# All expert pages inside the last 64 steps of a GRU, and a dense tail for the last 256 tokens

## The reference, cut to what matters

```
B, T, D = 4, 1024, 1024;  E = 8 experts, rank 128, top 2
h = cond_2048                                     # [4, 1024]
for t in range(1024):                             # GRU cell
    gi = x[:, t] @ W_ih + b_ih;  gh = h @ W_hh + b_hh
    r, z = sigmoid(i_r + h_r), sigmoid(i_z + h_z)
    n = tanh(i_n + r * h_n);     h = (1 - z) * n + z * h;   hs[:, t] = h
logits = hs / norm(hs) @ router_w                 # 4096 tokens
combine = top-2 of softmax(logits), renormalised, else 0    # [4096, 8]
out = x + sum_e combine[:, e] * (hs @ Wa[e] @ Wb[e])         # Wa 1024x128, Wb 128x1024
```

## Time and profile before

| | us |
|---|---|
| median of the runs | 9897.77 |
| the profiled execution | 9896.98 |
| its span, first to last instruction | 9895.2 |
| the last step's state stands (L865) | 9692.03 |
| from there to the end of the span | 203.2 |

### The profile page before, as it was taken

The page is one execution under the profiler, slowest core; times in us unless marked ns, Lnnn a source line. Parts: engine busy times, 40 slices in busy tenths (PEclk is TensorE's granted clock), DMA queues, the critical chain, the costliest instruction groups (busy, mean ns, idle before and its releaser), DMA issues.

```text
span 9895.2 us, 527046 instructions
## 1 busy us (share of the span) xinstructions
PE 9695.6 (98%) x229320; PEld 7286.9 (74%) x229320; DVE 5543.4 (56%) x29383; ACT 1236.8 (12%) x4796; POOL 512.9 (5%) x1207
## 2 busy tenths in 40 slices
PE   7999999999999999999999999999999999999995
PEld 5897778666788967767678887667888667769663
DVE  5555555555555555555555555555555555555662
ACT  2111111111111111111111111111111111111111
POOL 1000000000000000000000000000000000000001
PEclk9999999999999999999999999999999999999997
DMA  7121222212222122222223222222222222222225
GB/s 170 42 46 45 47 50 46 46 40 50 48 45 51 41 47 69 60 67 60 63 59 67 60 61 65 58 64 60 65 62 61 61 67 62 59 64 58 62 56 148
DMA packets 1425751, 606.69 MB, mean 61 GB/s; under 512 B 853856, under 2 KB 1377632, under 8 KB 1423392
## 3 DMA queue, kind: packets, MB, share of 16 engines
q1 hardware_dynamic: 1397792, 490.53, 21.8%
q0 software_dynamic: 25616, 82.18, 3.6%
HBM read 435.31 MB, written 164.96 MB: 61 GB/s over the span
## 4 chain that ended last, share of the span: by engine, by line
PE 94%; DVE 2%; DMA 2%; issue 1%; ACT 0%; SPq 0%; POOL 0%; DVEq 0%; POOLq 0%; ACTq 0%
PE gh_ps L1055 78%; PE gi_ps L1077 13%; DMA out<-w_hh_parts 1%; PE y_ps L1112 1%; PE y_ps L1124 1%; PE route_ps L1088 1%; DMA w_ih_tile<-in_L_cond_W_ih 1%; DVE gh L814 1%; DVE gh_sum L820 0%; ACT gate L976 0%; ACT cand L979 0%; DVE pre L827 0%; DVE zn L847 0%; DVE r_cand L835 0%; DVE cand_in L838 0%
## 5 line engine op out<-in xcount | busy, mean ns | idle before, releaser
L1055 PE MATMUL gh_ps<-w_hh_parts,h_parts 128*12 128x288 bf16 (+1 forms) x196608 | 8418.2, 326 | 41.6 <-DVE h_parts L865 23.0
L1055 PEld LDWEIGHTS gh_ps<-w_hh_parts,h_parts 128*12 128x12 bf16 x196608 | 6068.5, 88 | 2016.8 <-DVE h_parts L865 99.8
L814 DVE STREAM_TRANSPOSE gh<-gh_ps 128x288 f32<-128x288 f32 (+1 forms) x2048 | 1193.5, 583 | 2512.4 <-PE gh_ps L1055 2509.3
L1077 PE MATMUL gi_ps<-x_t,w_ih_tile 128*32 128x256 f32 x24576 | 1727.2, 380 | 41.6 <-DMA w_ih_tile<-in_L_cond_W_ih 41.6
L976 ACT ACTIVATE gate<-pre 128x24 f32<-128x24 f32 (+1 forms) x2048 | 471.1, 230 | 7291.2 <-DVE pre L827 7291.2
L1077 PEld LDWEIGHTS gi_ps<-x_t,w_ih_tile 128*32 128x32 f32 x24576 | 957.7, 110 | 410.3 <-DMA w_ih_tile<-in_L_cond_W_ih 47.4
L835 DVE TENSOR_TENSOR r_cand<-h_cand,gate 128x12 f32<-128x12 f32 (+1 forms) x2048 | 361.7, 177 | 602.8 <-ACT gate L976 602.8
L820 DVE TENSOR_REDUCE gh_sum<-gh 128x36 f32<-128x108 f32 (+1 forms) x2048 | 651.0, 318 | 71.1
L847 DVE TENSOR_TENSOR zn<-one_minus_z,cand 128x12 f32<-128x12 f32 (+1 forms) x2048 | 361.0, 176 | 412.3 <-ACT cand L979 396.1
L979 ACT ACTIVATE cand<-cand_in 128x12 f32<-128x12 f32 (+1 forms) x2048 | 441.7, 216 | 1110.1 <-DVE cand_in L838 1110.1
L860 DVE TENSOR_TENSOR h_parts<-shared,h_parts 128x12 bf16<-128x12 f32 (+1 forms) x2048 | 360.1, 176 | 162.9 <-DVE shared L855 14.0
(11 more groups left out here) (111 smaller groups left out, 1820.1 us busy)
## 6 DMA issues: line engine op xcount, KB each, us to landing
w_ih_tile<-in_L_cond_W_ih SPq DMA_DIRECT2D x1544, 128.0 KB, 2.9
gi_scratch<-gi_stage SPq DMA_DIRECT2D x384, 128.0 KB
gi<-gi_scratch SPq DMA_DIRECT2D x256, 192.0 KB, 4.4
x_raw<-expert_rows_of_h SPq DMA_DIRECT2D x220, 128.0 KB
shared<-wa_by_partition SPq DMA_DIRECT2D x55, 512.0 KB
expert_b<-in_L_ffn_Wb SPq DMA_DIRECT2D x55, 512.0 KB
x_raw<-in_x SPq DMA_DIRECT2D x272, 64.0 KB, 2.9
window_rows<-shared SPq DMA_DIRECT2D x132, 128.0 KB, 2.3
```

Source lines behind the costliest of these rows:

```text
L814: nc.vector.transpose(gh[k][:, :, :, :], ps[k][sp_][:, 0:GATES * n * Q].rearrange("p (q c i) -> p q c i", q=GATES, i=Q))\
L1055: ins = nc.tensor.matmul(ps[k_out][t % 2][j * Q:j * Q + SPLIT * B, 0:GATES * (o1 - o0) * Q], h_parts[:, (t - 1) % 2, c, :, :].rearrange("p ...
L1077: ins = nc.tensor.matmul(ps_i[m % 2][j * Q:(j + 1) * Q, 0:COLS], w_i[m % slots][:, c, j * Q:(j + 1) * Q], x_t[:, c, :, :].rearrange("p t b ...
```

## The change

Block 15 works off 23 pages in the place of ten: 15 that may be full (`ND`) and the 8 partly filled ones. They alternate between two sets of tiles (`set_of`: `raws`, `hts`, `was`, `wbs`, `uss`, `yrows`, `banks`; the second set lies in tiles that have no other use in that block). A piece of one page may now stand in the same step as a piece of the next. The last window but one (v = 31) and the last (v = 32), 256 tokens, are routed but not written into lists; the blank rows of the partly filled pages are filled in steps 12 to 19. After the recurrence `late_hidden` multiplies all 256 tokens, read straight from the ring, by each expert's Wa; VectorE scales the result by each token's weight for that expert (zero for most), and `late_output` sums all eight experts in PSUM. The weights are spread over the partitions by a matmul of ones with a diagonal. VectorE adds x, and SP writes `out` with plain DMAs.

In blocks 6 to 14 the output pieces of a page come one step earlier, and those of the fifth page go from steps 54 and 55 to 61 and 62.

```diff
-    return {"load": at(-2), "turn": at(0), "load_b": at(1), "u0": at(1), "u1": at(2), "take_u": at(2),
-            "y0": at(4), "y1": at(5), "finish": at(6),
-            "finished": at(8)}
-STEADY = turns([7, 17, 27, 40, 50])
-FINAL = turns([6, 11, 16, 21, 26, 31, 39, 44, 49, 54])
-LAST = 10
+    plan = {"load": at(-3), "load_a": at(-1), "turn": at(0), "load_b": at(1), "u0": at(1), "u1": at(2), "take_u": at(2),
+            "y0": at(3), "y1": at(4), "finish": at(5), "finished": at(6)}
+    for name, t in zip(("y0", "y1", "finish", "finished"), ends):
+        i = len(starts) - 1
+        plan[name] = {u: k for u, k in plan[name].items() if k != i}
+        plan[name][t] = i
+    return plan
+STEADY = turns([7, 17, 27, 40, 50], (61, 62, 63, 63))
+FINAL = turns([6, 9, 11, 13, 15, 18, 20, 22, 25, 27, 30, 32, 34, 37, 39, 42, 44, 46, 49, 51, 54, 56, 58])
...
+    LOOPED = (NB - 1 - FIRST) * PER
+    ND = FULL - LOOPED
+    LAST = ND + E
...
+        def set_of(k):
+            j = k - LOOPED
+            if j % 2:
+                return 1, j // 2, k - 2 if j > 1 else None
+            return 0, LOOPED + j // 2, k - 2 if j else k - 1
...
+            load_expert(0)
+            load_expert(1)
+            for h in range(2):
+                for b in range(B):
+                    sp.dma_start(z_x[h][b * Q:(b + 1) * Q, :], x[b, T - TB + h * WIN:T - TB + (h + 1) * WIN, :])\
+                      .then_inc(z_x_in[h], DMA)
             sp.wait_ge(mm_done[1], T)
...
+            sp.wait_ge(list_out, DMA * (4 * FLUSH + E))
+            for e in range(2, E):
+                load_expert(e)
+            for h in range(2):
+                for hf in range(2):
+                    here = slice(hf * HALF, (hf + 1) * HALF)
+                    sp.wait_ge(z_row_ready, 2 * h + hf + 1)
+                    for b in range(B):
+                        sp.dma_start(out[b, T - TB + h * WIN:T - TB + (h + 1) * WIN, here],
+                                     z_row[h][b * Q:(b + 1) * Q, here]).then_inc(z_out, DMA)
...
-            for q in range(NT):
-                pool.wait_ge(z_y_ready, 2 * (q + 1))
-                nc.gpsimd.indirect_dma_start(
-                    out=out_rows, out_offset=bass.IndirectOffsetOnAxis(ap=z_list[q % SETS][:, 0:1].bitcast(U32), axis=0),
-                    in_=z_row[q % 2], in_offset=None, bounds_check=B * T - 1, oob_is_err=False,
-                    compute_op=ALU.add).then_inc(y_out, DMA)
-                pool.wait_ge(y_out, DMA * (DONE + q + 1))
-                pool.sem_inc(z_free, 1)
+            weigh(2 * NB)
+            pool.wait_ge(y_out, DMA * DONE)
...
+            rank(2 * NB, 0, 1)
+            dve.wait_ge(consts, 2)
...
+            diagonal(0)
+            weights(2 * NB, 1)
+            diagonal(1)
+            for e in range(E):
+                dve.wait_ge(z_u_done, e + 1)
+                dve.wait_ge(scale_ready, 4)
+                if e >= 2:
+                    dve.wait_ge(z_y_done, e - 1)
+                nc.vector.tensor_tensor(z_us[e % 2], z_banks[e % 4][:, 0:2 * P],
+                                        z_scale[:, e, :, :].rearrange("p h n -> p (h n)"), ALU.mult).then_inc(z_us_ready, 1)
+            for h in range(2):
+                dve.wait_ge(z_x_in[h], DMA * B)
+                for hf in range(2):
+                    dve.wait_ge(z_y_done, E + 2 * h + hf)
+                    nc.vector.tensor_tensor(z_row[h][:, hf * HALF:(hf + 1) * HALF], ps[h][hf][:, :],
+                                            z_x[h][:, hf * HALF:(hf + 1) * HALF], ALU.add).then_inc(z_row_ready, 1)
...
+            for k, bank in enumerate(scale_banks):
+                act.wait_ge(scale_done, k + 1)
+                nc.scalar.activation(z_scale[:, k % 2 * 4:(k % 2 + 1) * 4, k // 2, :],
+                                     bank[:, :].rearrange("p (e n) -> p e n", n=P), ACT.Copy).then_inc(scale_ready, 1)
...
+            def late_hidden(e):
+                pe.wait_ge(z_wa_in[e], DMA)
...
+                for h in range(2):
+                    for c in range(NC):
+                        for j in range(NQ):
+                            ins = nc.tensor.matmul(
+                                z_banks[e % 4][j * Q:(j + 1) * Q, h * P:(h + 1) * P],
+                                z_wa[e][:, c * P + j * Q:c * P + (j + 1) * Q],
+                                window_at[1 - h][:, :, c, :].rearrange("p t b -> p b t"),
+                                start=(c == 0), stop=(c == NC - 1))
...
+            def late_output(e):
+                pe.wait_ge(z_wb_in[e], DMA)
+                pe.wait_ge(z_us_ready, e + 1)
+                for h in range(2):
+                    for hf in range(2):
+                        for j in range(NQ):
+                            ins = nc.tensor.matmul(
+                                ps[h][hf][j * Q:(j + 1) * Q, :], z_us[e % 2][:, h * P + j * Q:h * P + (j + 1) * Q],
+                                z_wb[e][:, hf * HALF:(hf + 1) * HALF], start=(e == 0), stop=(e == E - 1))
...
+            for e in range(4):
+                late_hidden(e)
+            for k, bank in enumerate(scale_banks):
+                pe.wait_ge(diag_ready, k // 2 + 1)
+                for j in range(NQ):
+                    ins = nc.tensor.matmul(bank[j * Q:(j + 1) * Q, :], ones[:, j * Q:(j + 1) * Q],
+                                           z_diag[k // 2][:, k % 2 * 4:(k % 2 + 1) * 4, :].rearrange("p e n -> p (e n)"),
+                                           start=True, stop=True)
+                ins.then_inc(scale_done, 1)
+            for e in range(E):
+                late_output(e)
+                if e + 4 < E:
+                    late_hidden(e + 4)
```

More of the change, by code:

```diff
@@ L236, in recurrence @@
[L236 to L239, removed]
+        comb = sb("weights", [P, 2, E])
+        x_flat = x_t[:, :, :, :].rearrange("p c t b -> p (c t b)")
+        raws = [raw, x_flat[:, 0:FB].rearrange("p (g f) -> p g f", g=NQ)]
+        hts = [ht, x_flat[:, FB:2 * FB].rearrange("p (c n) -> p c n", c=NC)]
+        was = [wa_x, w_i[0][:, :, :].rearrange("p c n -> p (c n)")]
@@ new lines, in recurrence @@
+        wbs = [wb_x[:, :], w_i[1][:, :, :].rearrange("p c n -> p (c n)")]
+        uss = [us, stage[0][:, 0:P]]
+        yrows = [yrow, nat]
+        ident, ones = stage[1][:, 0:P], stage[1][:, P:2 * P]
+        late = w[:, :, :, :].rearrange("p s c n -> p (s c n)").bitcast(FP32)
+        finite = late[:, 0:FB]
+        z_wa = [was[1], was[0]] + [late[:, 2 * e * FB:(2 * e + 1) * FB] for e in range(E - 2)]
+        z_wb = [wbs[1], wbs[0]] + [late[:, (2 * e + 1) * FB:(2 * e + 2) * FB] for e in range(E - 2)]
@@ L401, in load_b, with expert_of @@
[L401 to L404, removed]
+                sp.dma_start(list_n[i % PER], lists[bass.ds(row, P), :]).then_inc(list_in[tiles], DMA)
+            def expert_of(i, s):
+                return i - ND if i >= ND else \
+                    sp.value_load(base_at[s][:, 1, i:i + 1], min_val=0, max_val=E - 1)
@@ new lines, in load_a, with load_b @@
+            def load_a(k, i, s, tiles, held, before_k):
+                e = expert_of(i, s)
+                if before_k is None:
+                    sp.wait_ge(gi_done, NB * NM)
+                else:
+                    sp.wait_ge(u_done, before_k + (START + 1))
+                sp.dma_start(was[tiles], wa_dram[bass.ds(e * P, P), :]).then_inc(wa_in[tiles], DMA)
+            def load_b(k, i, s, tiles, held, before_k):
+                e = expert_of(i, s)
+                if before_k is None:
+                    sp.wait_ge(gi_done, NB * NM)
+                else:
+                    sp.wait_ge(y_done, before_k * 2 + (START + 2))
+                sp.dma_start(wbs[tiles], wb_rows[bass.ds(e * P, P), :]).then_inc(wb_in[tiles], DMA)
@@ L522, in _ @@
+            sp.wait_ge(z_out, DMA * 4 * B)
+            sp.wait_ge(x_copied, DMA * (NB - 1))
             for s in range(WL):
@@ new lines, in _ @@
+                    if last and t in AT_BLANK:
+                        after(n, t - 1)
+                        fill_blank(t - AT_BLANK[0])
+                    if last and t == AT_REST:
+                        pool.wait_ge(list_out, DMA * (4 * FLUSH + E))
+                        ts(base_at[TRIP][:, 0, ND:LAST], page[0:1, :], 1.0, 0.0, ALU.mult, ALU.add)
+                        pool.sem_inc(base_ready, 1)
+                        pool.wait_ge(gi_out[1], DMA * NB * NM // 2)
+                        link(nc.gpsimd.memset(ones, 1.0))
+                        link(nc.gpsimd.memset(ident, 0.0))
+                        link(nc.gpsimd.affine_select(out=ident, in_=ident, compare_op=ALU.not_equal, fill=1.0,
+                                                     base=0, pattern=[[-1, P]], channel_multiplier=1))
+                        pool.sem_inc(consts, 1)
@@ L920, in steps @@
                             transpose_x(n + 1, c)
-                    for k in range(2):
-                        part(n, t, k)
-                    if t in AT_ROWS:
```

(3 more changed lines are left out.)

414 lines of the change are left out of this document (182 added, 232 removed).

## The result

The changed kernel takes 9835.61 us, the median of four runs (9834.08 to 9836.51), against 9898.75 before (four runs; the 9897.77 further up is the median of three of them), with a ratio of 0.9936 (95% interval 0.9924 to 0.9948): 63 us faster. The forecast was 9826, with 9782 to 9868 as its range. The profiled execution takes 9834.08.

A forecast was written before the change was run, and what follows sets the result against it. TensorE was taken to bound the recurrence, and a row of 17 awaited write round trips the tail. From 9896.98 us, -7 (blocks 6 to 14), +33 (block 15) and -98 (tail) were summed to 9826; range 9782 to 9868.

The forecast's parts named there:

- The bound of the old tail: After the recurrence: 17 accumulating writes to `out`, each landing awaited, one in 8.8 us (1.55 issue, 7.3 landing).
- Blocks 6 to 14: Fifth page's last piece moves to step 62, which has room; other moves change nothing; -7 us over nine blocks.
- Block 15: 92 pieces instead of 40; a second piece in a step counts in full; +33 us (+28 to +39).
- The rival of waiting pieces: In block 15 each page holds TensorE by 1.5 us: +35 us, 9861 us; chance 0.12.
- The tail: After the recurrence: 203.2 us removed, 105.3 us added on one chain of TensorE, -98 us.
- The eight `late_hidden`: After the recurrence: eight expert products read from the ring, 8.0 us each, 64 us in all.
- The end: After the last output: add of x 0.7, four DMA issues 1.8, landing 2.3, together 4.8 us.
- The strided read: `late_hidden` reads elements 128 bytes apart: at least 240 ns a turn instead of 107; 8.0 us an expert taken.
- The extra of the logits' median: In `late_hidden`, 150 ns extra for 40 columns: 15.4 us an expert, 9885 us; chance 0.05 for 12 to 16 us.
- The rival of the free stride: In `late_hidden` strided reading costs nothing extra: 3.4 us an expert, 9789 us; chance 0.22.
- The half clock: Rival after the recurrence: clock at 0.50, outputs and scales double, +31 us, 9857 us; chance 0.08.
- The sum: Whole kernel, profiled execution: 9896.98 - 7 + 33 - 98, written as 9826 us.

The follow-up runs named there:

- e9: The kernel before, with the 17 writes of its last loop as plain indirect writes instead of accumulating ones: 9869.08 us, against 9897.73 beside it.
- e4: The changed kernel without the move of the fifth page's output pieces to steps 61 and 62 in blocks 6 to 14: 9837.63 us.
- e7: The changed kernel with each of the 23 VectorE transposes of a page's rows in block 15 done twice: 9831.92 us.
- e8: The changed kernel with the first piece of each of the 23 pages in block 15 done twice: 9852.65 us.
- e1: The changed kernel with `late_hidden` reading four neighbouring fp32 values before each jump, the diagonal, x and `out` reordered to match: 9800.78 us.
- e5: Like e1, plus scale matmuls after the second `late_hidden`, Wa loaded ahead of Wb, and fewer DMAs for x and `out`: 9787.48 us.
- e6: Like e5, but tiles of experts 4 to 7 loaded one expert after another, each after one more `late_hidden`: 9783.76 us.

## Why the prediction was right, and where its sizes were off

**The bound of the old tail** was read rightly off the chain; e9 shows the round trip by changing it. Its parts were read wrongly: the issue's 1.55 us is inside the 7.3 to landing, not in front of it. The 8.76 us of a write are 7.90 to landing in the mean and 0.87 from there to the next issue. That the two false terms gave 8.8 as well was luck, and the sum didn't use them.

**Blocks 6 to 14:** -7 forecast, -5.8 between the two traces and 7.0 to 10.0 by e4, depending on the trace set beside it, with step 62 at 8.70. That the moves of the other pieces change nothing holds to within 1.1 us, by which e4 is above the kernel before in these blocks.

**Block 15:** +33 forecast from 36, 20 and 8 steps of 9.53, 8.68 and 8.52; +33.9 measured, with medians of 9.53, 8.67 and 8.52. That TensorE's added work counts in full there, and VectorE's added transposes don't, is what e7 and e8 show; GpSimd and ScalarE weren't tested. The rival of waiting pieces did not come.

**The tail:** -98 forecast, -90.6 measured; here are the two terms that were too small. The eight `late_hidden` were put at 64 us (8.0 each). By their starts the last three take 7.9 to 8.1, as forecast, but the eight together 68.4: the first took 10.7 and the fifth 9.2, and in e4 and e8 again 10.6 to 10.8 and 9.1 to 9.2. The clock is at 0.50 until 9723.0, 1.2 us into the first, and loads of 412 GB/s run beside it; beside the fifth next to nothing runs (2 GB/s), at full clock. What slows the two stays open. The end was put at 4.8 us, with four issues behind the last output. There were 16 of 0.46 us each in a row that starts at 9823.17: the four quarters follow one another by 0.86 us and each has 1.85 of issues, so SP's queue had fallen behind. The end took 7.4. That the issues of the earlier quarters would still be in front was missed. The wait for the scales, 1.3, was 1.34.

**The strided read** was the largest doubt, worked out from the logits' least duration: 240 ns a turn, and 252 came. So the mechanism was right. That 8.0 was taken, where the rows allow 6.4 to 15.4, was a judgement, and that it came so near was in part luck. The extra of the logits' median (15.4 us an expert) was too much; that this is because those rows load strided weights beside was argued and not tested. The rival of the free stride (9789) is where the kernel stood once the stride was mended, 9783.76 to 9800.78 in e1, e5 and e6. The half clock did not come: 0.97.

**The sum** has a slip: 9896.98 - 7 + 33 - 98 is 9825, and 9826 was written, so each time that is built on it is 1 us too high. Of the 9 us that are left between 9825 and the 9834.08 of the profiled execution, about 7 are the tail's, and 1 each block 15's and blocks 6 to 14's.

## What to carry to other kernels

Before fp32 values are fed to TensorE straight from a ring, look at what lies within 16 bytes: reordering the columns of the result gave 35 us here, net of 2.7 for stores out of every fourth partition. Read the pace of a tail off the chain of waits: 17 writes, each waited for, cost 17 round trips, here 7.9 us and 0.87 between. And count the issues of a queue over the whole last stretch, not behind the last result alone.

## What the runs showed of the hardware

- TensorE reading fp32 columns in runs of one, two, four neighbours at a pitch of 128 bytes took 252, 133 and 109 ns a turn of four column groups at clock 1.00: 2.0 ns for each run until the columns' own 107 ns bind. That is the pace of later products; the first ones are slower, by up to a third with single values (10.7 us for 8.0). The durations showed it too: 440, 303 and 273 ns.
- While 6 MB of loads ran at about 400 GB/s, TensorE had holes of 0.6 to 2.5 us in the middle of matmuls that wait for no semaphore, eight in four kernels. Each ends 1.3 to 1.6 us after a 16 KB packet of the instruction queue has landed. Spaced loads took them away.
- An indirect write of 128 rows of 4 KB lands 6.3 us after the start of its issue plain and 7.3 accumulating (medians of 17), of which the issue on GpSimd is 0.96 and 1.55.
